# Comparison-matrix routing, a stacked 64-slot tile, and new instruction orders in a fused attention and mixture-of-experts kernel

## What is computed

```python
h = einsum('bhid,oi,od->bho', x, weighted_sum, weight)   # x (4,512,256,4)
h = concatenate([h, txt], axis=1)                        # (4, 544, 256)
h = h + gated_linear_attention(layernorm(h))             # 16 heads of 16, decay per channel
# mixture of experts over T = 2176 tokens, E = 8, K = 2, cap = 680
logits = clip(xf @ Wr, -1e4, 1e4)
top_v, top_i = top_k(logits, 2)
top_p = exp(top_v - max); top_p = top_p / (sum(top_p) + 1e-12)
pos = running count of tokens before this one at the same expert
kept = pos < cap
h_e = silu(xe @ W1[e]) * (xe @ W3[e])                    # D 256 -> F 1024
ye  = h_e @ W2[e]
out[token] += top_p * kept * ye
return h + out
```

## Time and profile before

| | |
|---|---|
| median of 3 runs | 643.94 us (641.04 to 644.14) |
| the profiled execution | 642.83 us, span of its instructions 641.1 us |
| mean granted TensorE clock | 0.955 of 2.4 GHz |
| busy share | PE 92%, weight loads 86%, VectorE 57%, ScalarE 52%, GpSimd 46% |
| chain that ended last | PE 84%, DMA 5%, DVE 4%, issue 3%, POOL 2% |
| by line in that chain | L1631 (three-product groups) 46%, L1673 (`down`) 18% |

### The profile page before, as it was taken

One profiled execution on the slowest core, in us unless ns is written; L12 is line 12 of the kernel. 1 busy time (PEld: TensorE's weight loads), 2 busy tenths in 40 slices (PEclk: granted clock), 3 DMA queues, 4 the chain that ended last, 5 costly groups with the idle time before them and its releaser, 6 DMA issues.

```text
span 641.1 us, 14355 instructions
## 1 busy us (share of the span) xinstructions
PE 592.0 (92%) x5062; PEld 553.3 (86%) x5062; DVE 364.5 (57%) x982; ACT 335.8 (52%) x887; POOL 296.5 (46%) x360
## 2 busy tenths in 40 slices
PE   5998999999999989824999999999999999999992
PEld 5997798789977866624999999999999999999991
DVE  5655677778568867771643635536356364463530
ACT  5587588447667735422644626537266273562520
POOL 5002122111624475742665657658575485665322
PEclk9999999999979988955999999999999999999997
DMA  7991101112400100316172360642715417143011
GB/s 209 306 291 69 43 18 50 34 58 79 137 5 30 62 21 1 109 52 211 52 241 35 90 176 9 196 80 51 208 16 173 102 33 223 19 108 36 3 18 25
DMA packets 43719, 58.98 MB, mean 92 GB/s; under 512 B 4864, under 2 KB 32272, under 8 KB 43664
## 3 DMA queue, kind: packets, MB, share of 16 engines
q1 hardware_dynamic: 36624, 48.94, 24.6%
q0 software_dynamic: 7040, 9.34, 8.2%
HBM read 40.73 MB, written 17.53 MB: 91 GB/s over the span
## 4 chain that ended last, share of the span: by engine, by line
PE 84%; DMA 5%; DVE 4%; issue 3%; POOL 2%; SPq 1%; ACT 1%; DVEq 0%; POOLq 0%
PE ps L1631 46%; PE ps L1673 18%; DMA sb_x_in<-in_x 3%; PE ps L1838 3%; PE ps L1797 3%; PE ps L1852 2%; PE ps L1833 2%; PE ps L1743 2%; PE ps L1649 2%; PE ps L1867 1%; PE ps L1813 1%; PE ps L1845 1%; PE ps L1807 1%; POOL xe_rows L908 1%; SPq L729 1%
## 5 line engine op out<-in xcount | busy, mean ns | idle before, releaser
L1631 PE MATMUL ps<-sb_xe_hi,sb_rounded 128*128 128x320 f32 (+1 forms) x1024 | 209.4, 299 | 0.0
L1631 PEld LDWEIGHTS ps<-sb_xe_hi,sb_rounded 128*128 128x128 f32 x1024 | 166.9, 190 | 1.3
L1631 PE MATMUL ps<-sb_xe_lo,sb_rounded 128*128 128x320 f32 (+1 forms) x512 | 151.7, 296 | 0.0
L1673 PE MATMUL ps<-sb_rounded,sb_h_hi 128*128 128x256 f32 (+1 forms) x640 | 117.4, 285 | 0.0
L1214 DVE TENSOR_TENSOR sb_dec<-ps,sb_gate 128x320 f32<-128x320 f32 (+1 forms) x128 | 58.5, 457 | 86.8 <-ACT sb_gate L966 86.8
L1631 PEld LDWEIGHTS ps<-sb_xe_lo,sb_rounded 128*128 128x128 f32 x512 | 97.5, 190 | 0.0
L1673 PEld LDWEIGHTS ps<-sb_rounded,sb_h_hi 128*128 128x128 f32 (+1 forms) x640 | 94.4, 178 | 0.0
L966 ACT ACTIVATE sb_gate<-ps 128x320 f32<-128x320 f32 (+1 forms) x128 | 52.1, 407 | 73.7 <-PE ps L1631 73.2
L1673 PE MATMUL ps<-sb_rounded,sb_h_lo 128*128 128x256 f32 (+1 forms) x320 | 89.9, 281 | 0.0
L832 POOL DMA_INDIRECT out_rows<-sb_att,sb_s_token x40 | 61.5, 1539 | 53.3 <-DVE sb_att L1228 47.5
L1221 DVE TENSOR_TENSOR sb_h_lo<-sb_dec,sb_h_hi 128x320 fp32r<-128x320 f32 (+1 forms) x128 | 73.8, 577 | 0.5
(11 more groups left out here) (181 smaller groups left out, 1019.7 us busy)
## 6 DMA issues: line engine op xcount, KB each, us to landing
sb_x_in<-in_x SPq DMA_DIRECT2D x16, 512.0 KB, 4.5
sb_raw<-in_L_ffn_W SPq DMA_DIRECT2D x16, 512.0 KB, 6.7
sb_x_in<-in_L_ffn_W SPq DMA_DIRECT2D x16, 512.0 KB, 4.4
sb_att<-xe_rows SPq DMA_DIRECT2D x40, 132.5 KB, 2.2
xe_rows<-sb_xr SPq DMA_DIRECT2D x3, 1457.5 KB, 15.9
sb_xn<-in_L_ffn_W SPq DMA_DIRECT2D x8, 512.0 KB, 4.7
sb_h<-in_L_ffn_W SPq DMA_DIRECT2D x8, 512.0 KB, 5.4
out_rows<-sb_h SPq DMA_DIRECT2D x16, 128.0 KB, 1.7
```

The source lines that it names most:

```text
L1631: ins = pe.matmul(out_ap, lhs, rhs, start=(i == 0), stop=(i == n - 1))
L1673: ins = pe.matmul(ps[BANK[s]][0:r, 0:D], hh[:, f, o:o + r], w2s[:, f, ww, :], start=(f == 0 and i == 0), stop=(f == FT - 1 and i == 2))
```

## The change

Five things. (1) `top2` compares all pairs of an expert's logits of a token at once: greater, equal and earlier, sum; an expert that fewer than two others beat is taken. One mask serves both experts. (2) Gates: a new step `shift` subtracts the maximum, `gate_exp` takes the exponential of all eight, `weigh` masks, sums and divides. (3) Ranks: a new step `limits` adds the round's counts to `cum` once; `rank` forms the running count over the chunks by one product of ones for each distance between chunks. `cum` starts at each expert's first row, and `slots` takes the larger and the sum minus the larger of a token's two rows. The table's unused rows now stand first (`ROW0`). (4) Experts: the 64-slot tile is the first. Its rows are loaded twice (two DMAs), into partitions 0 to 63 and 64 to 127. Of its hidden values the low part is written to columns 0 to 63 of `h_hi` and the high part to 64 to 127, all other columns moving up by 64, so that `down` multiplies 128 stationary columns with either part of w2: 16 products in place of 24. The two halves of the result are both scaled and both added to the output, the second by a step `scatter_low` after the third tile's. The first tile then also includes the product of the two low parts. (5) All five orders are laid out anew, and the second norm of image 3 goes in two batches in place of three.

The diff, cut; the orders are left out but for lines that the text speaks of.

```diff
@@ ACT_ORDER, between images 2 and 3
-decay_exp.2.0 x_turn.3.3.1 gate_proj.2.1.1 gate_silu.2 ln2_rsqrt.1.1 w13_split.0 embed.3.2 w13_split.1
-v_proj.2.2 w13_split.2 xn2_turn.1.2 exact.2 w13_split.3 w13_split.4 w13_split.5 xn2_turn.1.3 xn2_turn.1.4
-embed.3.3 ln1_rsqrt.3.0 w13_split.6 k_turn.2.0 ln1_rsqrt.3.1 w13_split.7 ln1_apply.3.4 k_turn.2.2 k_turn.2.1
+embed.3.3 exact.2 embed.3.2 w13_split.0 w13_split.1 xn2_turn.1.2 xn2_turn.1.3 k_turn.2.0 ln1_rsqrt.3.0
+ln1_apply.3.2 head_norm.2.0 xn_turn.3.2 v_proj.2.3 v_proj.3.0 v_proj.3.4 w13_split.2 state.2.2 w13_split.3
+gate_proj.3.0.1 w13_split.4 gate_proj.3.1.1 decay_proj.3.1.1 decay_proj.3.0.0 w13_split.5 w13_split.6
@@ DVE_ORDER, end of image 3
-ln2_newton.3.1 router.3.0 attn_out.3.4 ln2_stats.3.4 attn_out.3.3 ln2_stats.3.3 router.3.2 router.3.1 top2.3
-ln2_newton.3.2 weigh.3 slots.3 router.3.4 router.3.3 top2.4 weigh.4 slots.4 counts
+ln2_newton.3.0 og.3.4 attn_out.3.3 ln2_stats.3.3 attn_out.3.4 ln2_stats.3.4 router.3.0 router.3.1 ln2_newton.3.1
+router.3.2 shift.3 top2.3 weigh.3 limits.3 slots.3 router.3.3 router.3.4 top2.4 shift.4 limits.4 weigh.4 counts
+slots.4
@@
-LN2_BATCH = [[(0,), (1, 2), (3, 4)], [(0, 1), (2, 3, 4)], [(0, 1, 2), (3, 4)], [(0,), (1, 2), (3, 4)]]
+LN2_BATCH = [[(0,), (1, 2), (3, 4)], [(0, 1), (2, 3, 4)], [(0, 1, 2), (3, 4)], [(0, 1, 2), (3, 4)]]
@@ Cut
+        short = [width % P if width % P == P // 2 else P for width in widths]
+        self.tiles = [(at + max(0, r), min(P, r + P, width - r)) for (at, width), s in zip(self.halves, short)
+                      for r in range(s - P, width, P)]
+        self.twice = [n for n, (_, r) in enumerate(self.tiles) if r == P // 2]
+        self.lift = P // 2 * len(self.twice)
@@ expert_body
             steps += [("down", n), ("scatter", n), ("xe_turn", n)]
+            if n == 2:
+                steps += [("scatter_low", m) for m in self.twice]
@@ load_xe (SyncE)
+                    elif n in ex.cut.twice:
+                        for i in range(2):
+                            made(sp.dma_start(xe[i * r:(i + 1) * r, n, :], xe_rows[bass.ds(nxt * CAP + ROW0 + o, r), :]), "sp", s)
@@ h_split (VectorE)
+                    pieces = [(at, at + width, h_lo)]
+                    if lift and half == 0:
+                        pieces = [(lift, width, h_lo), (0, lift, h_hi)]
+                    for a0, a1, low in pieces:
+                        ins = dve.tensor_tensor(low[:, f, a0:a1], dec_flat[:, a0:a1],
+                                                h_hi[:, f, lift + a0:lift + a1].bitcast(F32), ALU.subtract)
@@ top2 (VectorE), all of it
+                    dve.tensor_tensor(more.rearrange(square, e=E, o=E), other, own, ALU.is_gt)
+                    link(dve.tensor_tensor(same.rearrange(square, e=E, o=E), other, own, ALU.is_equal))
+                    link(dve.tensor_tensor(same_c, same_c, before[...].to_broadcast([P, n, E * E]), ALU.mult))
+                    link(dve.tensor_tensor(more, more, same, ALU.add))
+                    link(dve.tensor_reduce(beats[:, 0:n, :], more.rearrange(square, e=E, o=E), AX.X, ALU.add))
+                    finish(dve.scalar_tensor_tensor(taken, beats, float(TOPK), valid, ALU.is_lt, ALU.mult), "dve", step)
@@ down (TensorE)
+                        if low_too:
+                            for ww in range(2):
+                                ins = pe.matmul(ps[BANK[s]][:, 0:D], h_hi[:, f, 0:2 * r], w2s[:, f, ww, :],
+                                                start=(f == 0 and ww == 0), stop=(f == FT - 1 and ww == 1))
+                            continue
@@ rank (TensorE)
-                    pe.matmul(bank[:, 0:(g1 - g0) * E], strict[:, :], work[:, 0:(g1 - g0) * E], start=True, stop=False)
-                    ins = pe.matmul(bank[:, 0:(g1 - g0) * E], ones[:, :],
-                                    cum[:, g0:g1, :].rearrange("p c e -> p (c e)"), start=False, stop=True)
+                    pe.matmul(bank[:, 0:n * E], strict[:, :], taken[:, 0:n * E], start=True, stop=False)
+                    for m in range(1, n):
+                        pe.matmul(bank[:, m * E:n * E], ones[:, :], taken[:, 0:(n - m) * E], start=False, stop=False)
+                    ins = pe.matmul(bank[:, 0:n * E], ones[:, :], cum[:, at[0]:at[0] + 1, :].to_broadcast([P, n, E]),
+                                    start=False, stop=True)
```

More of the change, by code:

```diff
@@ L90 @@
+attn_out.3.0@0 state.3.3@6 mix.3.2@4 attn_out.3.1@7 head_norm.3.2@5 scores.3.4 mix.3.3@4 attn_out.3.2@6
+head_norm.3.3@7 mix.3.4@5 head_norm.3.4@4 attn_out.3.3@6 attn_out.3.4@7 xn2_turn.3.0@5 xn2_turn.3.1@4
+xn2_turn.3.2@6 router.3.0@7 router.3.1@5 router.3.2@4 xn2_turn.3.4@7 router.3.4@5 xn2_turn.3.3@6 rank.3@4
+router.3.3@7 rank.4@6 counts@4
 """
 ACT_ORDER = """
[L93 to L94 removed]
@@ new lines @@
+ln2_newton.1.1 k_proj.2.1.1 ln1_stats.3.3 exact.2 ln1_stats.3.4 ln1_stats.3.2 scores.2.0 router.1.2 router.1.3
+ln1_newton.3.0 ln1_newton.3.1 state.2.0 router.1.4 shift.1 xn_turn.3.1 top2.1 limits.1 xn_turn.3.0 mix.2.0
+xn_turn.3.4 weigh.1 og.2.0 slots.1 xn_turn.3.2 state.2.1 xn_turn.3.3 attn_out.2.0 scores.2.1 ln2_stats.2.0
+scores.2.2 state.2.2 mix.2.1 scores.2.3 decay_sum.3.0 state.2.3 mix.2.2 og.2.1 scores.2.4 decay_sum.3.1 mix.2.3
+attn_out.2.1 ln2_stats.2.1 q_proj.3.1.0 q_proj.3.1.1 og.2.3 range.3 k_proj.3.0.0 og.2.2 attn_out.2.3
```

461 lines of the change are left out of this document (246 added, 215 removed).

## The result

| kernel | median us | runs | range | profiled execution (span) | granted clock of it |
|---|---|---|---|---|---|
| before | 642.54 | 20 | 640.78 to 644.14 | 642.83 (641.1) | 0.955 |
| after | 638.73 | 20 | 634.85 to 642.15 | 635.27 (633.5) | 0.964 |

The ratio is 0.9941 (0.9928 to 0.9954): 3.8 us faster, inside the range, but well under half of the 8.9 us of the sum. The profiled execution of after lies 3.5 us under its own median (one other of its 20 is as quick, 634.85), that of before 0.3 above its own. So the two profiles lie 7.6 us apart and are near the forecast, and the runs are not. Both differences have to be explained, and each has another cause.

A forecast was written before the change was run, and what follows sets the result against it. TensorE bounds the experts; small steps and scatters bound the passage and image openings. Terms -7.4 + 0.6 + 0.4 - 1.5 + 0 - 1.0 = -8.9 from the profiled 642.83 gave 633.9, raised to 634.5 us; range 629.0 to 640.5.

The forecast's parts named there:

- Bound: Whole kernel: TensorE bounds the expert blocks unbroken, so a product less is time off the end, eight times.
- D: Attention: TensorE left waiting at two new places and the clock falls, 7.1 us a place, 649.7 us; chance 3%.
- rival E: Experts' stacked tile: weight loads set its pace, +0.94 us an expert in place of -0.92, 649.4 us; chance 1%.
- F: Experts: counts read above 576 by an error, so the long form runs, near 695 us; chance 1%.
- The stacked tile: Experts' 64-slot tile: 16 products, 0.92 us less per expert, -7.4; late low part +0.6; sixth load +0.4.
- Rival A: Experts' first tile waits for VectorE's low part, half of the 0.92 lost per expert, 638.5 us; chance 13%.
- The sixth load: Passage: SyncE issues one more load for the first tile's rows, first turning later, +0.4 us (0 to 0.5).
- The passage: Between attention and experts: routing round 3 takes 5.65 us, 1.9 less; norm batching costs +0.4; net -1.5.
- Rounds 0 to 2: Routing in attention: round 0 +1.0 on TensorE, rounds 1 and 2 -0.5 each; together 0 (-3 to +3).
- the orders: Engines' new instruction lists: gain or loss at image openings, -4.5 to +4.5 us, taken as -1.0.
- The dip at image 2: Attention, 180 to 192 us: clock fall and idle time cost 4.5 us; expected gone or shorter, gain up to 4.5.
- rival C: Attention: dip at image 2 goes whole, VectorE's time in rounds 1 and 2 counts fully, 630.5 us; chance 14%.

The follow-up runs named there:

- the quick sets: Groups of kernels run together on one chip, nothing changed in the kernel before, which took 642.4 to 642.7 us there.
- the cheaper stacking: Changed kernel with VectorE's second subtraction replaced by a 64-wide ScalarE copy filling the stacked operand: 636.44 us beside 638.65 for the changed kernel.
- the runs behind 481 products: Kernels before and after, each with 481 unneeded TensorE products ahead of the first load: before 777.78 us (slow set), after 762.95 (slow) and 754.20 (quick).
- the slow sets: Groups of kernels run together on one chip, nothing changed in the kernel before, which took 666 to 667 us there.

## Why the prediction was right or wrong

**Bound, rivals D, E and F.** Right that the experts are one unbroken row of TensorE's: 0.9 us off a tile's products left the row for good. The stacked tile took 1.94 for the 1.90 of 16 x 0.1185. The loads of 128 columns are 188 ns long as before, for 135 with 64 columns. The Trainium skill (TensorE: Matmul & The Clock Gate, "Step-by-step: what each phase is for") says that a load's time goes by its columns; here it grows with them, by 1.39 and not by 2. Had the loads set the tile's pace, it would have been longer than 2.82; rival E is dead. The short form ran (five tiles to a body), so F is too.

**The stacked tile, -7.4 + 0.6 + 0.4.** The sum has 5.1 us too much: 8.9 for 3.8. This is the step that failed, -6.4 where the runs have -2.3 (alone) and -3.5 (on top of the rest), and it is mis-sized in three terms. (1) I asked for VectorE's second piece only at the first `down`, where it is the last slice's, and there it did no harm: the tile is 1.94 with nothing in front of it. But `h_split` is made eight times an expert, and each time the product that empties TensorE's bank stands behind it on VectorE. I gave the piece 0.19 us from a row in which GpSimd sent scatters and subtracted nothing; it takes 0.52 in the mean and 0.76 beside GpSimd's subtractions. That lengthened the six middle blocks by 0.34 to 0.68, 2.4 us in all, where I had 0.6 for the whole lateness of VectorE. Rival A had the mechanism (GpSimd's subtractions slow VectorE) and a price of 4, but the wrong place, so that "the row has VectorE free of other work there" could speak against it. The group of the product (L1214) in the profile of before had 46.4 us of idle time ahead of 64 of them, 0.7 each: room for 0.19, not for 0.76 when it comes on top of a first piece that GpSimd slows as well. (2) The sixth load: 0.8 for 0.4. (3) The end of the kernel: +0.7 that I had at 0. The scatter added cost nothing on GpSimd, but between the last scatter and the end it is 12.0 for 11.3 us. What the end waits for there is not shown. Sum -3.2 by the profile, measured -2.3 and -3.5.

**The passage, -1.5.** Round 3 was 5.82 us for a forecast of 5.65, and 1.6 to 1.7 shorter than before in every profile. The wait for `rank` that I had calculated is there (0.59 for 0.3). As a duration the step was right. As time off the end it was not, in the quick sets: -0.2 us. With the next term this is the second step that failed: passage and orders were to give -2.5 and gave -0.3.

**Rounds 0 to 2 and the orders, 0 and -1.0.** The dip at image 2 is shorter as forecast, 0.91 from 180 to 200 for 0.83. That at image 3, which I had staying, is shorter too and later: 1.00 and 0.83 in the ten us from 230 and from 240, for 0.79 and 0.70. This need not come from the orders: the kernel with the stacked tile alone has the old ones, and its one profile shows the same 1.00 and 0.83. (The diff has seven `w13_split` steps ahead of `k_turn.2.0`, not six, and two of them stay there.) So the profile goes part of the way to rival C, whose dip at image 2 was to go whole. The runs show nothing of it: the typical execution has 6 us more at 1.2 GHz than that of before in after, and 4 us more with routing and orders alone. That is worth up to 3 and 2 us, and about what the passage and the openings save. I named the dips as the unknown and gave ±4.5; what I missed is that they are not a property of the kernel alone. I read them off one execution each and added them up as if they were.

**The form of the sum.** A sum against one profiled execution is good for terms that the trace shows as unbroken work, as the bodies (the cheaper stacking: 2.0 us by the chains, 2.2 in the runs). The terms from half-speed stretches belong to that execution. Where the clock is concerned two profiles were 4 us further apart than the medians.

That the measured 638.7 is so near rival A's 638.5 is luck: A let passage and orders give their whole 2.5, and they gave 0.3. Still open: why TensorE has more time at the lower level in the ordinary executions of after than in its profiled ones. That earlier work of TensorE can do it is a hint from the runs behind 481 products, and that it tells these executions apart is only argued. Open too is what ScalarE and VectorE wait for in the slow sets, and what makes a set slow.

## What to carry to other kernels

Before adding an instruction to an engine, look at what stands behind it on that engine each time it runs, not only at who waits for its result, and price it beside its usual neighbour: a small VectorE instruction cost 0.22 us alone and 0.76 beside GpSimd's subtractions, and filling the operand by a copy on ScalarE gave the block its old 25.75 us back. A gain that is read from stretches at half clock is to be claimed only after several executions; compare mean granted clock and span of the runs with those of the profile first. Look also at what stands just ahead of a stretch before calling it free of waits. And measure an order of work in more than one set: the same lists were worth 0 in one and 9 us in another, where ScalarE stood for 8.4 us beside a row of ten scatters on GpSimd with the new lists and 10.9 with the old.

## What the runs showed of the hardware

- VectorE's 128x64 subtraction took 0.21 to 0.22 us in the 28 cases in which GpSimd subtracted nothing meanwhile, and 0.75 to 0.76 in the 36 in which it did; there was nothing in between. A 128x256 one took 0.41 or 0.55 and more, and 0.41 beside GpSimd too in the other half of the slots.
- The granted clock was 0.50 over the 10.2 us right behind a wait of TensorE of 2.40 us. Behind 481 extra products it was once also 0.88 over 10 us in which TensorE was busy without a gap, where it was 1.00 without them; these are two executions from different sets.
- In the slow sets an engine's wait without a visible releaser, up to 10.9 us long, ended within 2 us of the end of a row of GpSimd's indirect DMAs. The one of 7.7 us went away when the row was moved. In the quick sets there was none in any profile.
- One program took 642 us in some sets and 667 in others, nearly all of it in the part with many small instructions (23.3 of 24.4 us in after's profiles); the experts' bodies of each kernel were the same length in both.
- 16 products with 128 stationary columns took 1.94 us, 24 with 64 columns 2.82: 118 to 121 ns a product, whatever the columns.
